# A four-layer graph network on one core: visiting the two typed edge passes in fours on TensorE

## The reference

```
def _rgcn_conv(x, src, dst, edge_type, inv_deg, basis, comp, root, bias):
    xs = x[src]
    c = comp[edge_type]
    m = c[:, 0:1] * (xs @ basis[0])
    for b in range(1, basis.shape[0]):
        m = m + c[:, b:b + 1] * (xs @ basis[b])
    agg = jax.ops.segment_sum(m * inv_deg[:, None], dst, num_segments=n_nodes)
    return agg + x @ root + bias

h = jax.nn.relu(_rgcn_conv(h, src, dst, edge_type, inv_deg, basis1, comp1, root1, bias1))
x = x + _rgcn_conv(h, src, dst, edge_type, inv_deg, basis2, comp2, root2, bias2)
```

## Time and profile before

| what | value |
|---|---|
| median of 3 runs | 10746.02 us (10732.53 to 10749.62) |
| profiled execution: its time | 10738.4 us |
| its span | 10736.3 us |
| busy share of the span | PE 48%, DVE 42%, ACT 17%, POOL 60% |
| chain that ended last | another core or an unknown queue 37%, PE 23%, issue 18%, DVE 11%, POOL 4% |

### The profile page before, as it was taken

The page is one execution under the profiler, slowest core; times in us unless marked ns, Lnnn a source line. Parts: engine busy times, 40 slices in busy tenths (PEclk is TensorE's granted clock), DMA queues, the critical chain, the costliest instruction groups (busy, mean ns, idle before and its releaser), DMA issues.

```text
span 10736.3 us, 132836 instructions
## 1 busy us (share of the span) xinstructions
PE 5143.0 (48%) x35468; PEld 3759.8 (35%) x35468; DVE 4481.7 (42%) x9066; ACT 1867.5 (17%) x5090; POOL 6455.6 (60%) x6245
## 2 busy tenths in 40 slices
PE   3788477667676557777777311111112321111111
PEld 3677455555555435555555111111111111111110
DVE  7898555555555554444444221121112121111112
ACT  0677223323333200000000100000000100000000
POOL 8234555555555546666565566666666566666666
PEclk9999778888877778889888655555555655555555
DMA  6000133333333212222222222222221222222222
GB/s 260 23 15 15 36 88 95 93 92 94 93 92 92 79 44 65 64 63 64 65 64 62 82 58 56 56 57 59 56 58 56 87 58 56 57 56 58 57 58 56
DMA packets 501320, 736.15 MB, mean 69 GB/s; under 512 B 142419, under 2 KB 217811, under 8 KB 498372
## 3 DMA queue, kind: packets, MB, share of 16 engines
q0 software_dynamic: 199616, 212.17, 9.4%
q1 hardware_dynamic: 174060, 258.01, 7.7%
q10 hardware_dynamic: 127584, 265.22, 6.5%
HBM read 429.83 MB, written 305.03 MB: 68 GB/s over the span
## 4 chain that ended last, share of the span: by engine, by line
another core or an unknown queue 37%; PE 23%; issue 18%; DVE 11%; POOL 4%; DVEq 3%; ACT 2%; SPq 1%; DMA 1%; ACTq 0%; POOLq 0%
PE ps L1674 11%; DVE scn L1330 3%; PE ps L1738 2%; PE ps L1706 2%; PE ps L1583 2%; PE ps L1550 1%; POOL big L723 1%; PE ps L1555 1%; DVE picked_nodes L1266 1%; DVE idx L1292 1%; POOL big L786 1%; PE ps L1723 1%; PE ps L1649 1%; SPq L591 1%
## 5 line engine op out<-in xcount | busy, mean ns | idle before, releaser
L776 POOL DMA_INDIRECT gat<-typed_table,idx x3128 | 2996.7, 958 | 1591.4 <-issue 905.8
L776 POOL DMA_INDIRECT gat<-node_table,idx x2689 | 2626.6, 977 | 1845.0 <-issue 887.0
L1674 PE MATMUL ps<-big 128*128 128x320 bf16 x13230 | 2313.5, 331 | 627.3 <-issue 317.7
L1738 PE MATMUL ps<-ident,scn 128*128 128x128 f32 x3136 | 873.0, 370 | 3566.9 <-DVE scn L1330 2409.7
L1330 DVE TENSOR_TENSOR_SCAN scn<-flags,scn,ps 128x256 f32<-128x256 bf16 x1176 | 873.5, 743 | 3518.1 <-remote 3257.7
L1738 PEld LDWEIGHTS ps<-ident,scn 128*128 128x128 f32 x3136 | 533.5, 213 | 3869.6 <-issue 3847.2
L1674 PEld LDWEIGHTS ps<-big 128*128 128x128 bf16 x13230 | 1405.2, 109 | 1306.3 <-issue 450.9
L862 ACT COPY dmp<-ps 128x256 f32<-128x256 f32 x1568 | 578.9, 369 | 6295.8 <-remote 3966.9
L1706 PE MATMUL ps<-ident,gat 128*128 128x128 f32 x3136 | 820.9, 355 | 501.3 <-DVE gat L1297 310.7
L1266 DVE SCALAR_TENSOR_TENSOR picked_nodes<-node_ids,nodes_in_groups,ps 128x320 f32<-128x320 f32 x441 | 240.0, 544 | 1297.9 <-remote 749.3
L1706 PEld LDWEIGHTS ps<-ident,gat 128*128 128x128 f32 x3136 | 473.3, 177 | 646.0 <-issue 588.7
(11 more groups left out here) (289 smaller groups left out, 6037.9 us busy)
## 6 DMA issues: line engine op xcount, KB each, us to landing
scan_rows<-dmp ACTq DMA_DIRECT2D x784, 256.0 KB
flags<-keep_and_type_rows SPq DMA_DIRECT2D x980, 128.0 KB
spread_table<-tsl ACTq DMA_DIRECT2D x101, 576.0 KB, 16.0
shared<-spread_table SPq DMA_DIRECT2D x196, 288.0 KB
gat<-typed_table,idx POOLq DMA_INDIRECT x3128
gat<-node_table,idx POOLq DMA_INDIRECT x2689
typed_table<-shared SPq DMA_DIRECT2D x20, 1280.0 KB
group_rows<-node_group_rows SPq DMA_DIRECT2D x196, 128.0 KB
```

The source lines that it names most:

```text
L776: nc.gpsimd.indirect_dma_start(gat[:, k, g // ST, g % ST, :], None, table[:, :], bass.IndirectOffsetOnAxis(ap=idx[:, k, g:g + 1], axis=0)) ...
L1674: last = nc.tensor.matmul(product_bank(q, n), masks[:, n % 2, a, :], x3p[:, t, a, :, :].rearrange("p d b -> p (d b)"), start=a == 0 and t ...
L1738: last = nc.tensor.transpose(bank(2 + b1)[:, g * P:g * P + P], by_edge(scn[:, b1, :], g), ident[:, :])
```

## The change

It concerns q = 3 and 4 alone. PE goes through the pass in **visits of four superchunks** (`step_of_four`, only at the last of each four): eight transposes turn the rows of s - 3 to s, then eight turn back the scans of the four superchunks before those. Each superchunk still raises `s_turn` and `s_back` for itself. The eight banks of PSUM are cut into sixteen halves: `turned(n)` is one of eight halves in banks 0 to 3, `turned_back(n)` one in banks 4 to 7. The scans go to a ring of eight, `scr`, which lies in the room of the tile `oh` (free by then). DVE scans superchunk s - 4 at step s instead of s - 1 and waits for `s_turn` by pairs; ACT waits for `s_back` by pairs. The diff, without its empty lines:

```diff
--- before.py
+++ after.py
@@ -238,7 +238,18 @@
         acc = [a.bitcast(bf16).rearrange("p (j n) -> p j n", j=J + T)
                for a in (shared[:, 0:aw], big[:, x3w:x3w + aw])]
+        scr = oh[:, :, :, :, :].rearrange("p b q w i -> p (b q w i)").bitcast(f32).rearrange("p (n e) -> p n e", n=K)
         ps = ctx.enter_context(nc.psum_tensor("ps", [P, 8 * 512], f32))
+        def turned(n):
+            return ps[:, SH * n:SH * n + SH]
+        def turned_back(n):
+            return ps[:, SH * (K + n):SH * (K + n) + SH]
         def bank(n, w=512):
             return ps[:, 512 * n:512 * n + w]
@@ -857,10 +868,12 @@
                     if live(lag):
                         c1, n1 = lagged(c, n, lag)
                         k1 = n1 % KD
-                        act.wait_ge(s_back, nth(q) * NS + s - lag + 1)
+                        act.wait_ge(s_back, nth(q) * NS + s - lag + (2 - n1 % 2 if q > 2 else 1))
                         since(act, s_dump[k1 // 2], 16 * (nth(q) * NI * 2 + c1 * 2 + n1 // KD))
                         nc.scalar.copy(dmp[:, k1, :, :, :],
-                                       bank(2 + k1 % 2, G * D).rearrange("p (g t d) -> p t g d", g=GH, t=ST)
+                                       (turned_back(n1) if q > 2 else bank(2 + k1 % 2, G * D)
+                                        ).rearrange("p (g t d) -> p t g d", g=GH, t=ST)
                                        ).then_inc(s_evac, 1)
                         if k1 % 2:
@@ -1279,7 +1292,7 @@
                         mask_groups(q, s, 0, s)
                         if s == 0:
                             pick_nodes(q, 0, 0, 0)
-                link(v.memset(scn[:, 1, SH - 1:SH], 0.0))
+                link(v.memset((scr[:, K - 1, :] if q > 2 else scn[:, 1, :])[:, SH - 1:SH], 0.0))
                 if q == MLP:
                     dve.wait_ge(s_crs, 1)
                     v.tensor_copy(fil[:, 1, SH - 1:SH], bank(6, 1))
@@ -1316,7 +1329,16 @@
                         v.scalar_tensor_tensor(out=tpr[:, b, :], in0=typb[:, n % KD, :], scalar=typc[:, 0:1],
                                                in1=fit[:, b, :], op0=ALU.is_equal, op1=ALU.mult
                                                ).then_inc(s_tpr, 1)
-                    if live(1):
+                    if q > 2 and live(KD):
+                        c1, n1 = lagged(c, n, KD)
+                        dve.wait_ge(s_turn, nth(q) * NS + s - KD + 2 - n1 % 2)
+                        dve.wait_ge(s_keep[n1 // KD], flags_loaded(q, n1 // KD, c1 + 1))
+                        since(dve, s_scan, nth(q) * NS + s - KD)
+                        since(dve, s_back, nth(q) * NS + s - KD - K + 1)
+                        v.tensor_tensor_scan(scr[:, n1, :], keep8[:, n1, :], turned(n1),
+                                             scr[:, (n1 - 1) % K, SH - 1:SH], ALU.mult, ALU.add).then_inc(s_scan, 1)
+                    if q <= 2 and live(1):
                         c1, n1 = lagged(c, n, 1)
                         if q == MLP:
                             dve.wait_ge(s_zed, s)
@@ -1334,7 +1356,7 @@
                             s1, c1, n1, there = place(s, c, n, ahead)
                             if there and not (q == MLP and ahead == 1):
                                 work(q, s1, c1, n1)
-                eights(dve, step, 1, tail=1)
+                eights(dve, step, KD if q > 2 else 1, tail=1)
             dve.wait_ge(s_ax, 16)
@@ -1686,6 +1708,30 @@
                     pe.wait_ge(s_x3p, sum(len(BY_PRODUCT[o]) > 0 for o in range(1, q + 1)))
                     for s in range(2):
                         multiply_rows(s, 0, s)
+                def step_of_four(s, c, k, live):
+                    if k % KD != KD - 1:
+                        return
+                    if live(0):
+                        pe.wait_ge(s_scl, scaled * NS + s + 1)
+                        since(pe, s_scan, nth(q) * NS + s - (K - 1))
+                        pe.sem_inc(s_go_pe, 1)
+                        for n in range(k - KD + 1, k + 1):
+                            for g in range(GH):
+                                last = nc.tensor.transpose(by_edge(turned(n), g),
+                                                           gat[:, n, g, :, :].rearrange("p t d -> p (t d)"), ident[:, :])
+                            last.then_inc(s_turn, 1)
+                    if live(KD):
+                        pe.wait_ge(s_scan, nth(q) * NS + s - KD + 1)
+                        since(pe, s_evac, nth(q) * NS + s - KD - (K - 1))
+                        pe.sem_inc(s_go_pe, 1)
+                        for m in range(KD):
+                            n = (k + 1 + m) % K
+                            for g in range(GH):
+                                last = nc.tensor.transpose(turned_back(n)[:, g * P:g * P + P], by_edge(scr[:, n, :], g),
+                                                           ident[:, :])
+                            last.then_inc(s_back, 1)
                 def step(s, c, k, live):
                     b = k % 2
@@ -1739,7 +1785,10 @@
                                                        by_edge(scn[:, b1, :], g), ident[:, :])
                         last.then_inc(s_back, 1)
                     multiply_some(s, c, k, live, range(7 if mlp else 5, JA))
-                eights(pe, step, lag, tail=1)
+                if q > 2:
+                    eights(pe, step_of_four, KD, tail=1)
+                else:
+                    eights(pe, step, lag, tail=1)
             pe.wait_ge(s_tot, 1)
             nc.tensor.matmul(bank(6, 1), lower[:, :], csum[:, J - 1:J], start=True, stop=True).then_inc(s_pre, 1)
```

## The result

| | kernel before | changed kernel |
|---|---|---|
| median | 10751.03 us | 10737.38 us |
| range, runs | 10732.53 to 10772.86, 20 | 10724.06 to 10749.70, 20 |
| profiled execution, its span | 10738.4, 10736.3 us | 10744.7, 10741.6 us |

The ratio is 0.9986, with a 95% interval of 0.9981 to 0.9992: 14 us faster, where 121 were forecast. So the change does next to nothing: rival 4.

The account below looks back on a forecast made before the run. POOL's gathers, at 1.248 us each, plus 564 us of standstill on PE's late notices were taken to bound passes 3 and 4. Fewer stops (-132) and longer pass ends (+11) gave -121 us: 10625 us, range 10560 to 10850.

Parts of the forecast that it names:

- rival 4: Passes 3 and 4: POOL's standstill may depend only on the unchanged numbers of notices and gathers; 10746 within 21 us, 12%.
- What bounds the kernel: Passes 3 and 4: POOL gathers every 1.248 us and stands still 564 us beyond that, waiting for PE's late notices.
- 5.5 us a notice: Passes 3 and 4: while POOL gathers, each semaphore raise (notice) by PE arrives 5.5 us after the last, one after another.
- One stop per twelve superchunks, 6.6 us: Passes 3 and 4: POOL stops 32.7 times a pass at 6.6 us, against a 7.2 us pair per ten superchunks; 132 us saved.
- (1): Passes 3 and 4: POOL stops after eight superchunks instead of twelve; +93 us, 10839 us, 15%.
- (2): Passes 3 and 4: a stopped POOL frees queued notices one by one, 22 us a stop; +885 us, 11631 us, 9%.
- (3): Passes 3 and 4: the delay belongs to a PE visit, not a notice, so POOL never stops; -553 us, 10193 us, 8%.
- Drains: Ends of passes 3 and 4: catching up by four superchunks loses 5.55 us a pass, 11 us for both; less than 0 excluded.
- The rule: PE's notices in passes 3 and 4: at 26.3 ns each, 1568 cost 41 us, hidden; grouping neither wins nor loses. Not followed.

Follow-up runs that it names:

- held kind: Jobs where the unedited kernel before took 10703 to 10751 us and POOL stops in the typed passes; what makes a job so is open.
- second pair: The kernel before and the changed kernel, both unedited, measured again: 10702.91 and 10704.15 us, ratio 0.9999 (0.9990 to 1.0008).
- free kind: Jobs where the unedited kernel before took 9305 to 9312 us; traces of other kernels there show no POOL stops in the typed passes.
- first pair: The kernel before and the changed kernel as first measured for the result: medians 10751.03 and 10737.38 us, ratio 0.9986.

## Why the prediction was wrong

**What bounds the kernel: right.** POOL's pace of 1.248 us and the 564 us beyond it are confirmed: free of stops, a pass took 1951 to 1957 us, and the kernel before is 1.4 ms shorter with it (the other passes gain too).

**"5.5 us a notice": the step that failed.** The cycle was worked out from it: 28, 33, 39, 44, then four more to 66, a stop at 60. One start each 5.5 us is a fair reading of the earlier trace rows, but it isn't the price of a notice. A quarter of the notices cost as much in all, twice as many no more, and single ones waited 22 and 37 us. As far as the runs show, 2.8 us went with each transpose instead, and the change leaves their number alone. What holds them back stays open. From rows of one rate of notices I couldn't know whether the delay belongs to the notice, to the transposes or to POOL.

I also paired the rows wrongly. Counted off from the start of pass 3, the copy at 6716.42 and the scan at 6721.52 belong to these transposes, one superchunk before those that I named:

```profile
6701.18 0.68 PE L1738 MATMUL ps<-ident,scn 128*128 128x128 f32 x2 [7.43 <-DVE scn L1330]
6701.89 0.66 PE L1706 MATMUL ps<-ident,gat 128*128 128x128 f32 x2
```

So a notice was 14.6 and 19.0 us late there, behind others, and not 4 and 9.

**"One stop per twelve superchunks, 6.6 us": both terms mis-sized, and bound together.** It is one per sixteen (64 gathers), of about 11 us. The forecast had the four scans turned back announced 66 us after a restart; in the cycle shown ACT copies the last of them at 6758.27, 44 us after that at 6714.66. I priced a stop by a pair of the earlier trace rows less one restart, as if its length were fixed. It isn't: 7.2 us per 40 gathers before is 0.18 a gather, 11 per 64 is 0.17. More work between two stops goes with a longer stop. The earlier trace rows held the hint, since the second stop of a pair ended only when both made up 7 us.

**Rival 4, at 12%, was right**, though only half for its reason. The time that POOL stands still doesn't depend on how the notices queue. My argument against it was half right: at 6806.35 a stop did free all that waited, but only after standing longer. Of its two causes the notices are excluded by the quarter and the double; the gathers count, though not alone (183 us with half of them).

**The other rivals** didn't occur: no stops every 40 us (1), none of 15 us or more (2), and stops with two notices a visit as well, so that it isn't the visit that takes the delay once (3).

**Drains: right where POOL never stops,** 5.4 us for 5.55. In the held kind they don't show. In pass 3 of the changed kernel the first gather of scan rows follows the last gather, at 8284.79, after 13.14 us of idle time where the earlier trace rows has 18.35; in pass 4 it is 12.82 and 12.56. The second pair agrees: 14.48 and 12.88 where the kernel before has 18.24 and 14.87. I had excluded less than 0, and it is 5 to 6 us less for both passes. The kernel before ends pass 3 with a queue of late notices: ACT still waits on "remote" until 8281.92, 6.7 us after the last gather. That this covers the four superchunks' work is my reading, and no run tests it.

**The rule** of the Trainium skill (TensorE: Matmul & The Clock Gate, "The cost: per-tile semaphore tail", 26.3 ns an increment) agrees with the free kind, where doubling the notices leaves the passes at 1952 and 1957 us. In the held kind single notices waited up to 37 us, which it doesn't tell, and still its consequence held: grouping them neither wins nor loses.

**The 14 us** of the first pair are not located. The profiled executions stand the other way round (10738.4 and 10744.7 us), the passes differ by 3 us, the drains by 5, and the second pair shows no difference. Pass 3 begins 7 us later in the changed kernel in the first pair and 5 us earlier in the second, though passes 1 and 2 are the same program.

## What to carry to other kernels

When a wait looks as if it cost so much per event, vary the number of events alone before building on it; here a one-word edit (raise by 4 on the last) would have told that the grouping has nothing to win. When a producer stops now and then, divide the length of its stops by the work between them: if that ratio stays when the work between them grows, the stops only become rarer and longer. And time a kernel in more than one job before a difference is put down to the code.

## What was not expected

- The same program takes 9305 to 9312 us in some jobs and 10703 to 10751 in others, on the same two chips: 15% (10703 / 9305), far more than any edit that kept the result did.
- In the held kind PE's notices are late while POOL gathers every 1.248 us. At 1.335 us, with a fill between gathers, they come within 0.03 us.
- In the held kind many register and semaphore instructions of some engines take 0.7 us and more where they take 0.02 to 0.09 in the free kind: DVE's and SP's in the changed kernel, SP's above all in the kernel before, POOL's and SP's with the fill (where a pass is still 195 us above its pace). So PE's late notices look like one face of something that slows several engines, rather than its cause. What it is I can't tell from these traces.
